# One order of three engines changed: a layer's value products ahead of the query projection, its block transposes behind the next maxima

## The chip, the cores and the metric

The kernel runs on one core of a Trainium2 chip. The metric is the device time of one execution in microseconds. A core has five engines that run their own instruction streams and meet through semaphores: TensorE (PE in the profile; PEld is its weight loads), VectorE (DVE), ScalarE (ACT), GpSimd (POOL) and SyncE (SP, which here issues the DMAs). TensorE writes only to PSUM, which has eight banks; ACT and DVE read results from there.

## The reference, cut to what matters

The output is x plus a dense low-rank attention of the normalised x plus a stack of six layers. The change lies in the layers alone, so only they are shown. T is 2048 tokens, a layer has 16 heads of 64, a local attention over windows of 32 tokens (each sees its own window and the one before), and a gated feed-forward part.

```
def attn_layer(x, Wqkv, qs, ksc, Wo):
    qkv = x @ Wqkv
    q, k, v = jnp.split(qkv, 3, -1)
    q = l2norm(q) * qs
    k = l2norm(k) * ksc
    q = q * cos * scale + rotate_half(q) * sin * scale
    k = k * cos * inv + rotate_half(k) * sin * inv
    out = local_attention(q, k, v)
    return out @ Wo
...
for i in range(DEPTH):
    x = attn_layer(shift_tokens(x), Wqkv[i], q_scale[i], k_scale[i], Wo[i]) + x
    x = ffn_layer(shift_tokens(x), ln_g[i], ln_b[i], W1[i], b1[i], W2[i], b2[i]) + x
```

## The kernel before

The first third of the time (part A of the kernel) is the dense attention. Part B, from about 770 us on, is the six layers. A layer is cut into 16 tiles of 128 tokens, 96 tiles in all, and the feed-forward part into chunks of four tiles. Each engine runs one hand-written loop over a turn number `u`; in every turn it does one step each for several tiles at different stages. On PE, turn `u` makes the scores of tile u-3, the q, k and v projections of tile u-1, the values' products (probabilities times v) and the output product of tile u-5, and the transposes of q and k ("turns", `L1342`) of tile u-2. Every engine works through its list strictly in the written order, so a wait of one step holds all steps written behind it.

The lines that matter, by engine:

- PE: scores `L1362` (mask `L1357` ahead of them), projections `L1316` to `L1318` (six matmuls each for q, k and v, `w_qkv` and `x_cut` in the name), values `L1378` (64 matmul records), output `L1390`, turns `L1342` (four transposes each: k_turn0, q_turn0, q_turn1, k_turn1, in that order), mean `L1399`, feed-forward products `L1316` with `xl_cut`, down product `L1429`.
- ACT: squares of q and of k `L754`, values_out `L796` (copies the values' bank to `o_T`), 16 exponentials `L805`, q_T `L776` and k_T `L785`/`L788`, v `L815`, gelu `L882`.
- DVE: maxima of the scores `L1069`, blocks `L1061` (a 32 by 32 transpose of the probabilities, `pc<-pr`), rotation of q or k: cosine `L1038`, sums of squares `L1020`, two sine halves `L1049`, `L1050`; residual `L1093`/`L1094`, sums of the probabilities `L1076`, deviation from the mean `L1101`, gate `L1147`.
- SP: eight DMAs `L471` carry the blocks to `xy`, from which the values' products read.

PSUM banks are given out by a table, and whoever takes a bank waits until its last user is read out:

```
BANKS = {"q": ((4, 5), (4, 5)), "k": ((2, 3), (2, 3)), "v": ((0, 1), (4, 5)),
         "q_turn0": ((4,), (4,)), "q_turn1": ((1,), (5,)), "k_turn0": ((6,), (6,)),
         "k_turn1": ((0,), (7,)), "values": ((6, 7), (6, 7)), "output": ((7,), (7,)),
         "score": ((0, 1), (0, 1)), "mean": ((7,), (7,)), "var": ((4,), (4,)),
         "up0": ((4, 5), (4, 5)), "up1": ((2, 3), (2, 3)), "up2": ((6, 7), (6, 7)),
```

Two of its consequences are used below. q_turn0 takes bank 4 right after q of the same turn, so it waits for `q_out`, the second sine half of q's rotation on DVE. And the values take banks 6 and 7, whose last user is up2 of the feed-forward part (read by the gate on DVE, `up_out2`), the mean (read by the deviation on DVE, `mean_out`), the down product or the output, in turns of four.

A chunk's steps fall into four kinds of turn, which repeat: a turn with the mean (A below), one with variance and down product (B), one without any (C), one with the three up products (D). The round read below is A from 1647.69 us, B from 1661.23, C from 1676.69 and D from 1690.19 to 1706.65, each from one start of the scores to the next.

Of the kernel before, what the change touches and what calls it, by code (L numbers as in the profile page):

```python
# [100 lines left out]
def tile(x):  # L101
    return x if 0 <= x < END else None


def chunk(x):
    c, r = divmod(x - 3, 4)
    return c if r == 0 and 0 <= c < CHUNKS else None


def dense_turn(x):  # L110
    g, r = divmod(x - 22, 8)
    return g if r == 0 and 0 <= g < NC else None


def late(x):
    c = chunk(x)
    return c if c is not None and c >= CHUNKS - NC else None
# [15 lines left out]
def bank_users():  # L133

    users, last = {}, {}

    def take(stage, unit):
        if unit is not None:
            of = BANKS[stage][unit % 2]
            users[stage, unit] = [last[b] for b in of if b in last]  # L140
            last.update({b: (stage, unit) for b in of})

    for u in range(FIRST, LAST):
        take("score", tile(u - 3))
        take("finish", late(u - 12))
        take("q", tile(u - 1))
        take("values", tile(u - 5))
        take("k", tile(u - 1))
        take("output", tile(u - 5))
        take("k_turn0", tile(u - 2))  # L150
        take("q_turn0", tile(u - 2))
        take("q_turn1", tile(u - 2))
        take("mean", chunk(u - 5))
        take("k_turn1", tile(u - 2))
        take("v", tile(u - 1))
        take("up0", chunk(u - 8))
        take("up2", chunk(u - 8))
        take("var", chunk(u - 6))
        take("down", chunk(u - 10))
        take("att", dense_turn(u))  # L160
        take("up1", chunk(u - 8))
    return users
# [583 lines left out]
def scalar_b(e, w, m, s):  # L746
    banks = Banks(m, s)

    def squares(u, i):
        if u is None:  # L750
            return
        w.wait_ge(s[f"proj{i}"], u + 1)
        w.wait_ge(s[f"ss{i}"], u)
        e.activation(m.nrms[i][:, :].rearrange("p (a b) -> p a b", a=2), banks.two("qk"[i], u),  # L754
                     ACT.Square).then_inc(s[f"sq{i}"], 1)

    def root_estimate(u):
        if u is None:
            return
        r = m.rs[u % 2]  # L760
        w.wait_ge(s["q_scaled"], u - 1)
        w.wait_ge(s["k_scaled"], u - 1)
        w.wait_ge(s["rB_arg"], u + 1)
        e.activation(r[1][:, :], r[0][:, :], ACT.Ln).then_inc(s["rB_ln"], 1)
        w.wait_ge(s["rB_ln"], u + 1)
        e.activation(r[2][:, :], r[1][:, :], ACT.Exp, scale=-0.5).then_inc(s["rB_exp"], 1)
        w.wait_ge(s["rB_exp"], u + 1)
        e.activation(r[1][:, :], r[2][:, :], ACT.Square).then_inc(s["rB_sq"], 1)

    def turned_q(u, hf):  # L770
        if u is None:
            return
        bank = banks.one(f"q_turn{hf}", u).rearrange("p (a b) -> p a b", b=P)
        w.wait_ge(s[f"turn0{hf}"], u + 1)
        w.wait_ge(s["score_mm"], u)
        e.activation(m.q_T[:, 4 * hf:4 * hf + 4, :], bank, ACT.Copy).then_inc(s[f"qT_out{hf}"], 1)  # L776
# [14 lines left out]
    def values_out(u):  # L791
        if u is None:
            return
        w.wait_ge(s["pv_mm"], u + 1)
        w.wait_ge(s["y_mm"], u)
        e.activation(m.o_T[:, :, :].rearrange("p (g j) i -> p g (j i)", g=2), banks.two("values", u), ACT.Copy).then_inc(s["oT_out"], 1)  # L796
# [96 lines left out]
    for u in range(FIRST, LAST):  # L893
        exponentials(tile(u - 4))
        squares(tile(u - 2), 1)
        turned_q(tile(u - 3), 0)
        turned_q(tile(u - 3), 1)
        turned_k(tile(u - 3), 0)
        turned_k(tile(u - 3), 1)
        keep_v(tile(u - 2))  # L900
        deviation_squares(chunk(u - 6))
        high_ln(chunk(u - 8))
        ln_root_estimate(chunk(u - 7))
        dense_output(dense_turn(u - 1))
        gelu_table(chunk(u - 9))
        gelu(chunk(u - 9), 0)
        high_x(tile(u))
        gelu(chunk(u - 9), 1)
        gelu(chunk(u - 9), 2)
        root_table(chunk(u - 9))  # L910
        scale_shift(chunk(u - 8))
        root_estimate(tile(u - 2))
        squares(tile(u - 1), 0)
        values_out(tile(u - 5))

# [92 lines left out]
def vector_b(e, w, m, s):  # L1010
# [19 lines left out]
    def rotate_cos(u, i):  # L1030
        if u is None:
            return
        n, raw = "qk"[i], banks.two("qk"[i], u).rearrange("p a (h d) -> p (a h) d", d=DH)
        w.wait_ge(s[f"sq{i}"], u + 1)
        w.wait_ge(s["rt"], u + 1)
        w.wait_ge(s[f"turn{i}0"], u - 1)
        w.wait_ge(s[f"turn{i}1"], u - 1)
        e.tensor_tensor(view(m.tcs[u % 2][i][:, :]), raw, wide(m.rt[u % 2][:, 2 * i, :], DH), ALU.mult).then_inc(s[f"rot{n}_c"], 1)  # L1038
# [17 lines left out]
    def blocks(u):  # L1056
        if u is None:
            return
        w.wait_ge(s["pnorm"], u + 1)
        w.wait_ge(s[f"moved{u % 2}"], 128 * (u // 2))  # L1060
        e.transpose(m.pc[u % 2][:, :, :, :].rearrange("p w h c -> p (w h) c"),  # L1061
                    m.pr[u % 2][:, :, :, :].rearrange("p w h c -> p (w h) c")).then_inc(s["pT"], 1)

    def maxima(u):
        if u is None:
            return
        w.wait_ge(s["score_mm"], u + 1)
        w.wait_ge(s["smexp"], u)
        e.tensor_reduce(m.mxB[:, 0, :], banks.two("score", u).rearrange("p a (b c) -> p (a b) c", c=2 * WIN), AX.X, ALU.max,  # L1069
                        negate=True).then_inc(s["sm_max"], 1)  # L1070
# [126 lines left out]
    for u in range(FIRST, LAST):  # L1197
        gated(chunk(u - 9), 2)
        final_sum(late(u - 11))
        ln_root_slope(chunk(u - 7))  # L1200
        maxima(tile(u - 3))
        rotate_cos(tile(u - 1), 0)
        square_sums(tile(u - 1), 0)
        rotate_sin(tile(u - 1), 0)
        ln_root_fix(chunk(u - 7))
        residual_1(tile(u - 5))
        prob_sums(tile(u - 3))
        low_ln(chunk(u - 8))
        rotate_cos(tile(u - 1), 1)
        prob_reciprocals(tile(u - 3))  # L1210
        rotate_sin(tile(u - 1), 1)
        if u == 6:
            sums_reciprocal()
        dense_norm(dense_turn(u))
        final_add(late(u - 11))
        square_sums(tile(u - 1), 1)
        root_argument(tile(u - 1))
        gated(chunk(u - 8), 0)
        gated(chunk(u - 8), 1)
        deviation(chunk(u - 5))  # L1220
        add_epsilon(chunk(u - 6))
        blocks(tile(u - 3))
        residual_2(chunk(u - 10))
        first_scale(chunk(u - 6))

# [86 lines left out]
def tensor_b(e, w, m, s):  # L1312
# [7 lines left out]
    def project(u, which):  # L1320
        if u is None:
            return
        bank, xc = banks.two("qkv"[which], u), m.x_cut[u % 2]
        w.wait_ge(s["x_hi"], u + 1)
        w.wait_ge(s["x_lo"], u + 1)
        w.wait_ge(s[f"ld_wqkv{which}"], 32 * (u // NT + 1))
        banks.wait_free(w, "qkv"[which], u)
        for hf in range(2):
            o = which * INNER + hf * CH
            mm = cut_product(bank[:, hf, :], [xc[:, k, :] for k in range(2)], [m.w_qkv[:, k, o:o + CH] for k in range(2)])  # L1330
        mm.then_inc(s[f"proj{which}"], 1)
# [107 lines left out]
    def finish(c):  # L1439
        if c is None:  # L1440
            return
        bank = banks.one("finish", c).rearrange("p (j f) -> p j f", f=P)
        w.wait_ge(s["fin_sum"], c % NC + 1)
        banks.wait_free(w, "finish", c)
        for j in range(CH // P):
            o = c % NC * CH + j * P
            t = e.transpose(bank[:, j, :], m.att[:, o:o + P], m.ident[:, :])
        t.then_inc(s["fin_T"], 1)

    for u in range(FIRST, LAST):  # L1450
        score(tile(u - 3))
        finish(late(u - 12))
        project(tile(u - 1), 0)
        values(tile(u - 5))
        project(tile(u - 1), 1)
        output(tile(u - 5))
        turn(tile(u - 2), 1, 0)
        turn(tile(u - 2), 0, 0)
        turn(tile(u - 2), 0, 1)
        mean(chunk(u - 5))  # L1460
        turn(tile(u - 2), 1, 1)
        project(tile(u - 1), 2)
        up_product(chunk(u - 8), 0)
        up_product(chunk(u - 8), 2)
        variance(chunk(u - 6))
        down_product(chunk(u - 10))
        dense_output(dense_turn(u))
        up_product(chunk(u - 8), 1)
# [62 lines left out]
```

## Time and profile before

| what | value |
|---|---|
| runs (three) | median 2306.8 us, 2303.33 to 2308.38 |
| profiled execution, its own time | 2294.56 us |
| its span, first to last instruction | 2292.8 us |
| granted TensorE clock, mean of the span | 0.971 of full speed |
| PE / DVE / ACT / POOL busy | 92% / 86% / 77% / 57% of the span |
| tiles, values' products, block transposes | 96 each |

The table is read so: the span is what the trace covers, the profiled execution lies 12 us below the median of the runs, and a busy share is a mean over both parts. A busy share of PE counts modelled ends of pipelined matmuls, so two neighbours overlap in the rows, and the start of the next one says more than the end of the last.

### The profile page before, as it was taken

The page shows a single profiled execution, that of the slowest core. Times are in us where ns is not written, and L with a number is a line of the kernel's source. Part 1 is how long each engine was busy: PE and PEld are TensorE (multiplying, and loading weights), DVE is VectorE, ACT ScalarE, POOL GpSimd, SP SyncE. Part 2 cuts the span into 40 slices and gives each one's busy share as a digit, 9 for nine tenths or more (in the row PEclk, how much of TensorE's full clock was granted, in tenths as well). Part 3 has the DMA queues.
Part 4 walks back from the last instruction along what each step waited for, and adds up shares of the span by engine and source line. Part 5 has one row for each costly group of instructions (what it writes and reads, how often), then busy time and mean ns, then how long its engine had stood idle before and what let it go on. Part 6 is the DMA issues. An engine that isn't in the chain of part 4 may idle for free. (4 is left out here: it accounts for less than half of the span.)

```text
span 2292.8 us, 69755 instructions
## 1 busy us (share of the span) xinstructions
PE 2105.6 (92%) x28217; PEld 1292.7 (56%) x28313; DVE 1981.1 (86%) x2378; ACT 1774.5 (77%) x4234; POOL 1316.2 (57%) x1088
## 2 busy tenths in 40 slices
PE   5999999999997689999999999999999999899985
PEld 2122222222222467777777777776777777777773
DVE  7999999999990789988998989888898989898973
ACT  3388888888887478878878878887887888788873
POOL 4211111111100888887877878788787888788860
PEclk8699999999999799999999999999999999999998
DMA  2322222222220233343425333433334433433331
GB/s 44 96 65 78 72 73 78 70 82 49 60 69 16 54 84 85 93 128 95 102 72 142 94 93 88 130 98 82 85 92 116 104 88 85 125 88 100 90 79 41
DMA packets 167654, 194.06 MB, mean 85 GB/s; under 512 B 87398, under 2 KB 107364, under 8 KB 167332
## 3 DMA queue, kind: packets, MB, share of 16 engines
q1 hardware_dynamic: 167076, 189.59, 31.5%
q8 instruction: 223, 3.65, 0.7%
q14 instruction: 99, 0.81, 0.1%
q10 hardware_dynamic: 256, 0.00, 0.0%
HBM read 56.91 MB, written 25.42 MB: 36 GB/s over the span
## 5 line engine op out<-in xcount | busy, mean ns | idle before, releaser
L988 DVE TENSOR_REDUCE mx<-S_ps 128x1 f32<-128x1024 f32 x512 | 601.6, 1219 | 24.8 <-PE S_ps L1270 19.1
L736 ACT ACTIVATE PT<-E_ps 128x512 f32<-128x512 f32 x1024 | 533.4, 602 | 101.4 <-PE E_ps L1279 98.9
L642 POOL TENSOR_TENSOR tc<-tc,ts 128x1024 f32<-128x1024 f32 x192 | 464.4, 2419 | 34.5 <-DVE ts L1050 34.0
L650 POOL TENSOR_TENSOR tc<-tc,rs 128x1024 f32<-128x1024 f32 x192 | 362.0, 1907 | 13.8
L1270 PE MATMUL S_ps<-KS,QS 48*128 48x512 bf16 x1024 | 320.5, 399 | 9.9 <-DVE mx L988 4.7
L805 ACT ACTIVATE pr<-B_ps,mxB 128x64 f32<-128x64 f32 x1536 | 325.0, 372 | 2.6 <-DVE mxB L1069 2.6
L1279 PE MATMUL E_ps<-QS,KS 64*128 64x512 bf16 x1024 | 316.8, 382 | 7.4 <-ACT PT L736 5.2
L584 POOL CAST w_cut_b<-w_raw_b 128x512 fp32r<-128x512 f32 (+1 forms) x48 | 27.6, 576 | 511.3 <-DMA w_raw_b<-in_Wqkv 379.1
L1316 PE MATMUL B_ps<-w_qkv,x_cut 128*128 128x512 f32 x576 | 260.9, 453 | 26.1 <-POOL x_cut L597 9.2
L1038 DVE TENSOR_TENSOR tc<-B_ps,rt 128x1024 f32<-128x1024 f32 x192 | 234.8, 1223 | 45.2 <-ACT nrm L754 31.9
L1287 PE MATMUL O_ps<-PT,va 128*32 128x512 f32 x2048 | 273.7, 606 | 0.0
L1279 PEld LDWEIGHTS E_ps<-QS,KS 64*128 64x128 bf16 x1024 | 79.3, 93 | 338.2 <-ACT PT L736 259.0
L604 POOL TENSOR_TENSOR pr<-pr,mxB 128x1024 f32<-128x1024 f32 x96 | 184.0, 1917 | 142.2 <-DVE mxB L1083 142.2
L754 ACT ACTIVATE nrm<-B_ps 128x1024 f32<-128x1024 f32 x192 | 208.6, 1086 | 54.0 <-PE B_ps L1318 52.0
L1318 PE MATMUL B_ps<-w_qkv,x_cut 128*128 128x512 f32 x576 | 231.7, 402 | 0.4 <-issue 0.4
L1317 PE MATMUL B_ps<-w_qkv,x_cut 128*128 128x512 f32 x576 | 232.1, 403 | 0.0
L1020 DVE TENSOR_REDUCE ss<-nrm 128x16 f32<-128x1024 f32 x192 | 232.0, 1208 | 0.0
L1342 PE MATMUL B_ps<-ident,tc 128*128 128x128 f32 x1536 | 202.2, 277 | 23.4 <-DVE ts L1050 9.3
L1378 PE MATMUL B_ps<-xy,vs 128*64 128x64 f32 x3072 | 195.0, 227 | 21.2 <-issue 11.1
L1342 PEld LDWEIGHTS B_ps<-ident,tc 128*128 128x128 f32 x1536 | 172.7, 142 | 51.1 <-issue 19.0
L1378 PEld LDWEIGHTS B_ps<-xy,vs 128*64 128x64 f32 x3072 | 166.6, 140 | 58.0 <-issue 57.9
L1390 PEld LDWEIGHTS B_ps<-o_T,w_o 128*128 128x128 f32 x1536 | 187.6, 193 | 14.1 <-ACT o_T L796 6.2
(179 smaller groups left out, 3982.0 us busy)
## 6 DMA issues: line engine op xcount, KB each, us to landing
xy<-pc SPq DMA_DIRECT2D x768, 64.0 KB, 2.0
vs<-v SPq DMA_DIRECT2D x96, 384.0 KB, 3.7
Wqkv_cut<-w_cut_b SPq DMA_DIRECT2D x72, 256.0 KB, 2.4
w_qkv<-Wqkv_cut SPq DMA_DIRECT2D x36, 512.0 KB, 7.2
rot<-in_rot SPq DMA_DIRECT2D x96, 128.0 KB, 2.6
vs<-v SPq DMA_DIRECT2D x96, 128.0 KB, 3.8
w_raw_b<-in_Wqkv SPq DMA_DIRECT2D x36, 256.0 KB, 2.9
W_cut<-w_cut_b SPq DMA_DIRECT2D x24, 170.5 KB, 2.5
```

Source lines behind the costliest of these rows:

```text
L642: e.tensor_tensor(tc[:, :], tc[:, :], m.ts[i][:, :], ALU.add).then_inc(s[f"rot{n}"], 1)
L650: e.tensor_tensor(tc, tc, m.rs[u % 2][2][:, i * H:(i + 1) * H].unsqueeze(2).to_broadcast([P, H, DH]), ALU.mult).then_inc(s[f"{n}_scaled"], 1)
L736: e.activation(m.PT[n % NPT][:, :], turns.bank("probs", n)[:, :], ACT.Exp).then_inc(turns.sem("probs", n), 1)
L805: a = e.activation(pb[:, :, h, :], sc[:, h, :, :], ACT.Exp, bias=m.mxB[:, 0, h:h + 1], scale=1.0)
L988: e.tensor_reduce(m.mx[h % 2][:, i, hf:hf + 1], m.S_ps[n % 2][:, :, :], AX.XY, ALU.max).then_inc(s["sc_max"], 1)
L1038: e.tensor_tensor(view(m.tcs[u % 2][i][:, :]), raw, wide(m.rt[u % 2][:, 2 * i, :], DH), ALU.mult).then_inc(s[f"rot{n}_c"], 1)
L1270: mm = e.matmul(m.S_ps[n % 2][:, c, :], m.QS[sl][rows, i * P:(i + 1) * P], m.KS[sl][rows, k:k + CH], start=True, stop=True)
L1279: e.matmul(turns.bank("probs", n)[:, :], m.KS[sl][rows, j * P:(j + 1) * P], m.QS[sl][rows, chunk_cols(c)], start=True, stop=True).then_inc ...
L1287: e.matmul(m.O_ps[VC * c:VC * (c + 1), :], m.va[:, j, h, :], m.PT[n % NPT][:, :], start=(j == 0), stop=(j == NT - 1)).then_inc(s["pv"], 1)
L1316: e.matmul(bank, left[0], right[0], start=True, stop=False)
L1342: t = e.transpose(bank[:, j, :], m.tcs[u % 2][i][:, b * P:(b + 1) * P], m.ident[:, :])
L1378: mm = e.matmul(bank[at, j, :, b, :], v[:, d:d + DH], m.xy[u % 2][:, b, :, par * NP + j, :], start=(b == 0 and j % (NP // 2) == 0), stop=T ...
```

## The change

Four lists are rewritten, with no instruction added or removed. PE makes the values' products right behind the scores, and q's and k's projections stand next to each other behind them; the table of bank users follows. ACT copies the values out before it squares q. DVE does the block transpose of a tile one place later, behind the maxima of the next tile.

```
 def bank_users():
...
         take("score", tile(u - 3))
         take("finish", late(u - 12))
+        take("values", tile(u - 5))
         take("q", tile(u - 1))
-        take("values", tile(u - 5))
         take("k", tile(u - 1))
...
 def scalar_b(e, w, m, s):
...
         root_estimate(tile(u - 2))
+        values_out(tile(u - 5))
         squares(tile(u - 1), 0)
-        values_out(tile(u - 5))
...
 def vector_b(e, w, m, s):
...
         maxima(tile(u - 3))
+        blocks(tile(u - 4))
         rotate_cos(tile(u - 1), 0)
...
         add_epsilon(chunk(u - 6))
-        blocks(tile(u - 3))
         residual_2(chunk(u - 10))
...
 def tensor_b(e, w, m, s):
...
         score(tile(u - 3))
         finish(late(u - 12))
+        values(tile(u - 5))
         project(tile(u - 1), 0)
-        values(tile(u - 5))
         project(tile(u - 1), 1)
```

On PE, this is the order in a turn of kind A before, from the scores to the second transposes of q; the brackets name the semaphores that a row waits for.

```order
L1362 MATMUL B_ps<-k_T,q_T 32x64 x64
L1316 MATMUL B_ps<-w_qkv,x_cut 128x512 [waits up_out0,x_lo,x_hi]
...
L1378 MATMUL B_ps<-xy,vs 64x2x32 [waits up_out2,shift1,moved1]
...
L1316 MATMUL B_ps<-w_qkv,x_cut 128x512 [waits up_out1]
...
L1390 MATMUL B_ps<-o_T,w_o 128x128 [waits oT_out]
...
L1342 MATMUL B_ps<-ident,tc 128x128 [waits k_scaled]
...
L1342 MATMUL B_ps<-ident,tc 128x128 [waits q_out,q_scaled]
...
L1342 MATMUL B_ps<-ident,tc 128x128 [waits smexp]
```

The two `L1316` rows are q's and k's projection. This is the same piece of the changed kernel.

```order
L1362 MATMUL B_ps<-k_T,q_T 32x64 x64
L1378 MATMUL B_ps<-xy,vs 64x2x32 [waits up_out2,shift1,moved1]
...
L1316 MATMUL B_ps<-w_qkv,x_cut 128x512 [waits up_out0,x_lo,x_hi]
...
L1316 MATMUL B_ps<-w_qkv,x_cut 128x512 [waits up_out1]
...
L1390 MATMUL B_ps<-o_T,w_o 128x128 [waits oT_out]
...
L1342 MATMUL B_ps<-ident,tc 128x128 [waits k_scaled]
...
L1342 MATMUL B_ps<-ident,tc 128x128 [waits q_out,q_scaled]
...
L1342 MATMUL B_ps<-ident,tc 128x128 [waits smexp]
```

The values moved up by one projection, with their wait for `up_out2`; between q's projection and the row that waits for `q_out` there now stand only k's projection, the output product and one set of transposes.

On DVE, these are the rows from the end of a turn of kind D into one of kind A before: gate, blocks, gate, maxima and the rotation of q.

```order
L1147 SCALAR_TENSOR_TENSOR hid<-B_ps,b,gel 128x512 [waits gelu1]
L1061 STREAM_TRANSPOSE pc<-pr 128x1024 [waits moved0,pnorm]
L1147 SCALAR_TENSOR_TENSOR hid<-B_ps,b,gel 85x512 [waits gelu2]
L1069 TENSOR_REDUCE mxB<-B_ps 128x16 [waits score_mm]
L1038 TENSOR_TENSOR tc<-B_ps,rt 128x1024 [waits turn00,turn01,rt,sq0]
```

And this is the same place in the changed kernel.

```order
L1147 SCALAR_TENSOR_TENSOR hid<-B_ps,b,gel 128x512 [waits gelu1]
L1147 SCALAR_TENSOR_TENSOR hid<-B_ps,b,gel 85x512 [waits gelu2]
L1069 TENSOR_REDUCE mxB<-B_ps 128x16 [waits score_mm]
L1061 STREAM_TRANSPOSE pc<-pr 128x1024 [waits moved0,pnorm]
L1038 TENSOR_TENSOR tc<-B_ps,rt 128x1024 [waits turn00,turn01,rt,sq0]
```

The block transpose moved behind the third gate and the maxima; the rotation of q still waits for its squares (`sq0`) from ACT.

## Rows read from the trace of the kernel before

**Rows 1.** Stretches A, B, D, sum: length, busy PE PEld DVE ACT POOL, clock, DMA.

```profile
1647.69:1661.23 13.54, 13.06 (x246) 10.50 (x246) 11.85 (x17) 12.23 (x32) 10.12 (x9) 1.00 0.36 90
1661.23:1676.69 15.46, 15.40 (x253) 11.71 (x253) 14.18 (x20) 11.36 (x32) 14.20 (x13) 1.00 0.32 80
...
1690.19:1706.65 16.46, 16.39 (x263) 13.22 (x263) 14.69 (x20) 14.57 (x37) 14.97 (x13) 1.00 0.30 75
sum 58.96, PE 57.31 PEld 45.58 DVE 54.07 ACT 50.23 POOL 50.10; mean PE 14.33 PEld 11.39 DVE 13.52 ACT 12.56 POOL 12.52
```

**Rows 2.** Timeline of PE in turn A: start, length, instruction, [idle before].

```profile
1649.11 0.50 PE L1316 MATMUL B_ps<-w_qkv,x_cut 128*128 128x512 f32 x1
...
1650.75 0.34 PE L1378 MATMUL B_ps<-xy,vs 128*64 128x64 f32 x4
...
1652.77 0.50 PE L1316 MATMUL B_ps<-w_qkv,x_cut 128*128 128x512 f32 x1
...
1654.27 1.95 PE L1390 MATMUL B_ps<-o_T,w_o 128*128 128x128 f32 x16
...
1660.93 0.38 PE L1357 MATMUL B_ps<-mask_bf,ident_bf 128*128 128x512 bf16 x1 [0.33 <-ACT k_T L788]
```

**Rows 3.** Timeline of PE in turns C and D.

```profile
1687.60 0.50 PE L1316 MATMUL B_ps<-w_qkv,x_cut 128*128 128x512 f32 x1 [0.31 <-ACT q_T L776]
...
1689.88 0.38 PE L1357 MATMUL B_ps<-mask_bf,ident_bf 128*128 128x512 bf16 x1 [0.62 <-ACT k_T L788]
...
1692.87 0.40 PE L1318 MATMUL B_ps<-w_qkv,x_cut 128*128 128x512 f32 x1
...
1695.21 0.50 PE L1316 MATMUL B_ps<-w_qkv,x_cut 128*128 128x512 f32 x1
...
1698.52 1.95 PE L1342 MATMUL B_ps<-ident,tc 128*128 128x128 f32 x16
```

**Rows 4.** Timeline of DVE, end of turn A's rotation and the same in D.

```profile
1654.73 0.68 DVE L1050 TENSOR_TENSOR ts<-B_ps,rt 128x512 f32<-128x512 f32 x1
1656.25 0.28 DVE L1093 TENSOR_TENSOR stream<-B_ps,stream 64x128 f32<-64x128 f32 x1 [0.84 <-PE B_ps L1390]
...
1657.22 1.22 DVE L1076 TENSOR_REDUCE mxB<-pr 128x16 f32<-128x1024 f32 x1 [0.37 <-ACT pr L805]
...
1662.76 0.69 DVE L1101 TENSOR_TENSOR xl<-stream,B_ps 128x512 f32<-128x512 f32 x1 [0.18 <-issue]
...
1697.23 0.68 DVE L1050 TENSOR_TENSOR ts<-B_ps,rt 128x512 f32<-128x512 f32 x1
```

**Rows 5.** Timeline of DVE around the block transpose between D and A.

```profile
1648.74 1.24 DVE L1061 STREAM_TRANSPOSE pc<-pr 128x1024 f32<-128x1024 f32 x1
1649.90 0.71 DVE L1147 SCALAR_TENSOR_TENSOR hid<-B_ps,b,gel 85x512 f32<-85x512 f32 x1
```

**Rows 6.** Timeline of ACT in turn A.

```profile
1647.35 1.49 ACT L882 ACTIVATE gel<-B_ps,b 128x512 f32<-128x512 f32 x2 [0.17 <-PE B_ps L1318]
```

**Rows 7.** Timeline of DVE, a late rotation of q in another turn.

```profile
1376.82 0.68 DVE L1050 TENSOR_TENSOR ts<-B_ps,rt 128x512 f32<-128x512 f32 x1
```

**Rows 8.** Timeline of PE, waits of two kinds elsewhere in part B.

```profile
1377.65 1.50 PE L1342 MATMUL B_ps<-ident,tc 128*128 128x128 f32 x12 [1.68 <-DVE ts L1050]
...
2033.60 0.34 PE L1378 MATMUL B_ps<-xy,vs 128*64 128x64 f32 x4 [1.34 <-DVE xl L1101]
```

**Rows 9.** Timeline of PE in the first turn of a layer.

```profile
1726.77 0.27 PE L1378 MATMUL B_ps<-xy,vs 128*64 128x64 f32 x1 [2.91 <-issue]
```

**Rows 10.** Busy time by stretch after two long stalls of PE (columns as in group 1).

```profile
1726.80:1730.70 3.90, 3.90 (x58) 3.49 (x59) 1.42 (x3) 1.37 (x4) 3.90 (x3) 0.61 0.80 194
1862.00:1867.00 5.00, 2.66 (x67) 2.28 (x66) 4.97 (x4) 1.16 (x2) 4.69 (x5) 1.00 0.58 110
```

**Rows 11.** Timeline of DVE near the end of part B.

```profile
2226.49 1.25 DVE L1061 STREAM_TRANSPOSE pc<-pr 128x1024 f32<-128x1024 f32 x1 [0.50 <-POOL pr L604]
...
2232.48 1.23 DVE L1069 TENSOR_REDUCE mxB<-B_ps 128x16 f32<-128x1024 f32 x1
```

More of the change, by code:

```diff
@@ L145, in bank_users @@
         take("finish", late(u - 12))
+        take("values", tile(u - 5))
         take("q", tile(u - 1))
-        take("values", tile(u - 5))
         take("k", tile(u - 1))
@@ L912, in scalar_b @@
         root_estimate(tile(u - 2))
+        values_out(tile(u - 5))
         squares(tile(u - 1), 0)
-        values_out(tile(u - 5))
 def vector_a(e, w, m, s):
@@ L1201, in vector_b @@
         maxima(tile(u - 3))
+        blocks(tile(u - 4))
         rotate_cos(tile(u - 1), 0)
@@ L1221, in vector_b @@
         add_epsilon(chunk(u - 6))
-        blocks(tile(u - 3))
         residual_2(chunk(u - 10))
@@ L1452, in tensor_b @@
         finish(late(u - 12))
+        values(tile(u - 5))
         project(tile(u - 1), 0)
-        values(tile(u - 5))
         project(tile(u - 1), 1)
```

## The prediction

> **What bounds the kernel now.** I read first the busy times of four neighbouring turns, because the six layers are one round of four turns said again and again. A turn runs from one start of the scores to the next; A, B, C and D are named in the text ahead. TensorE is busy for 57.31 of the round's 58.96 us, VectorE for 54.07, so PE is the nearest to a bound, and DVE has 4.89 us to spare [rows 1]. Second, I read PE's timeline for what it stands at. In B and D it hardly stands at all (15.40 of 15.46 and 16.39 of 16.46 [rows 1]), so there whatever holds PE is paid in full. In A and C it waits shortly before the next scores for ACT's copies of k (0.33 in A, 0.62 in C), and in C for the copies of q too (0.31) [rows 2, 3]: there a stall of PE can in part be taken out of these waits. Third, I read DVE's and ACT's timelines in the same turns for what PE's banks are waiting for, and last two places of part B where such a wait already happens.
>
> **The change part by part.** No instruction is added. The price, if any, is in waits.
>
> *The query's bank.* q_turn0 takes bank 4 from q of the same turn, and waits until DVE has done the second sine half of q's rotation. In turn D, q's last matmul ends at 1692.87 + 0.40 = 1693.27 [rows 3] and that sine half at 1697.23 + 0.68 = 1697.91 [rows 4]. So the chain squares on ACT, cosine, sums, two sine halves on DVE takes 4.64 us. How soon PE goes on after it is seen where PE did wait for it: the sine half ends at 1376.82 + 0.68 = 1377.50 [rows 7], the transposes start at 1377.65 [rows 8], 0.15 later. On PE, from the start of k's projection (1695.21) to q_turn0 pass 3.76 us: k_turn0 starts at 1698.52, and its four of 16 transposes in 1.95 us take 0.45 [rows 3]. Before the change, the values' products stood between q's end and k's start, 2.02 us (1650.75 to 1652.77 [rows 2]), and the chain was just covered. After it, k starts right behind q. A product of six matmuls takes 1.50 (1652.77 to 1654.27 [rows 2]), 0.25 each, and the last one is 0.40 long [rows 3], so q ends 0.15 after k's start. q_turn0 then starts 0.15 + 4.64 + 0.15 = 4.94 after k's start instead of 3.76: **1.18 us later in each turn**. From this goes the seam between q and values: q's product lasts 1.64 to the start of the values (1649.11 to 1650.75), k's 1.50 [rows 2], so 0.14 may be saved where values no longer follow a projection; it may also come back behind the scores, where no row shows such a seam. I take it as saved, 1.04 net; the bounds are 1.04 and 1.18.
>
> *What is left of it.* In D all of it, 1.04. In C, PE's waits of 0.31 and 0.62 hide most, and 0.2 is left (bounds 0 and 1.18).
>
> *Values ahead of q in A.* The values take banks 6 and 7 from up2, and wait for the third gate on DVE. The block transpose no longer stands ahead of that gate (1648.74 [rows 5]); its gelu ends at 1647.35 + 1.49 = 1648.84 [rows 6], the gate takes 0.71 [rows 5], and with the 0.15 the values can start at 1649.70. The scores leave PE at 1649.11, where q started [rows 2]. So PE stands 0.59 where q's projection used to cover the wait. k then starts at 1649.70 + 2.02 + 1.50 = 1653.22 instead of 1652.77, 0.45 later, and q_turn0 0.45 + 1.18 = 1.63 later. PE's 0.33 ahead of the next scores hides a part, which leaves between 0.45 and 1.30. I take the middle, 0.9.
>
> *Values ahead of q in B.* Here they take bank 7 from the mean, so they wait for the deviation on DVE, a wait that another turn of B shows already, 1.34 us long [rows 8]. With k at 1653.22 in A, q's end is 1653.37 and q's rotation ends at 1658.01, where it ended at 1654.73 + 0.68 = 1655.41 [rows 4]. Behind it come the two residual adds (0.28 and about as much) and the sums of the probabilities, now at 1658.6 instead of 1657.22, 1.4 later. From there to the deviation DVE has no gap but 0.18 [rows 4], so the deviation ends at 1662.76 + 0.69 + 1.4 = 1664.85, and the values can start at 1665.0. The scores of B leave PE 13.54 [rows 1] after those of A, at 1662.65, and 0.9 later now, at 1663.55. PE stands 1.45. Together with the 1.04 of the query's bank, B is longer by 2.5 (bounds 1.04 and 3). ACT's copy of the values has a whole projection more time, so the output product loses nothing.
>
> *Maxima ahead of blocks.* The maxima start up to 1.24 sooner, the transpose's length [rows 5], and gain nothing: ACT's exponentials stand behind the squares of q, which now come last (before: behind values_out, in the same place). The blocks come later by the maxima and by what stands between, up to two ops of the feed-forward part. They feed the values two turns on, through eight DMAs; the moves and the first use lie more than a turn apart, so I cost it at nothing, and at up to 2 us in each of B's turns if that cover is gone. SP's loads of rotation tables and of a new layer's weights stand behind these moves and come about 2 us later, but so does the projection that needs them.
>
> *Ends.* In the first turn of a layer PE stands 2.91 us anyway between q and k (it stands at nothing that the profile shows, while weights load) [rows 9]. This covers B's 2.5 in five turns: -12.5. Near the end the blocks of the last tile but one move from 2226.49 behind the maxima at 2232.48 [rows 11], 6 us; the tail's values feel some of it: between 0 and 6, I take 3.
>
> *Sum.* A round: 0.9 + 2.5 + 0.2 + 1.04 = 4.64. Values and q share a turn in 92 turns (96 tiles; the first four turns have no values, the last four no q), 23 rounds: 106.7. Less 12.5, plus 3: 97. Against the profiled execution's own 2294.6 that is 2391.6. The runs shown have their median 12.2 above that execution, so I put the 97 on the median: 2306.8 + 97 = **2404 us**, 4.2% slower.
>
> A rule to weigh against this: PE is busy for 57.31 us of the round, its weight loads for 45.58 and DVE for 54.07 [rows 1]. The Trainium skill, Perfetto Trace Analysis, section Identifying the Most-Contended Engine, says that the busy share of matmuls is a poor measure, that weight loads should be taken instead, and that the engine with the highest occupancy is the one that counts. By that rule DVE is the bound here, and a change that adds no work to it costs only what its 4.89 us of idle time can't take up; the sum would then be near 0. The rows of B and D, in which PE never stands, speak against reading it so.
>
> **The rivals.**
>
> *Only the bank, no waits of the values.* If DVE and ACT run ahead again by the next turn, the values find their banks free: A 0.45, B 1.04, C 0.2, D 1.04, 2.7 a round, 62 in 23 rounds, less 5 in the first turns of layers, plus 3: 60, 2367. For it: in D nothing waits for such a bank. Against it: DVE's sums start 1.4 later by its own order.
>
> *No change.* DVE takes up what is lost: the two long holds of A and B, 0.59 + 1.45 of PE and the 2 x 1.18 behind, come to 4.4, which fits into DVE's 4.89 [rows 1]. This needs PE to be ahead of DVE on the average, so that a hold moves idle time and adds none: 2307. Against it: PE stands nowhere in B and D.
>
> *Faster.* The seam of 0.14 is saved in 92 turns, 13 us, and the query's rotation is through in time: 2294. That needs the chain of 4.64 to shrink below 3.46 (3.76 less 0.15 and 0.15). DVE's part can start sooner, since the blocks wait no longer ahead of it, but in turn D it starts right behind the squares, so nothing of the kind is free. The price decides from 1.2 us on.
>
> *Clock.* After a stall of 2.91 us [rows 9] the granted clock of the next 3.9 us is 0.61, so it fell to its lower level, 1.2 GHz, for most of it; a stretch with 2.34 us of standing, 2.66 busy of 5.00, kept 1.00, 2.4 GHz [rows 10]. If the new stalls of B bring the clock down in each round, the stretch of 3.9 us loses 0.39 of itself, 1.5 us: 23 x 1.5 = 35 more, 2440. The Trainium skill, TensorE: Matmul & The Clock Gate, section Why this matters for your kernels, warns of idle gaps between bursts of matmuls in this way. [...]
>
> **How the numbers follow.** Chances: the forecast (2380 to 2425) 0.55; only the bank (2345 to 2380) 0.2; clock, or more waits (above 2425) 0.12; slightly slower (2312 to 2345) 0.03; no change 0.05; faster 0.05. The range 2350 to 2435 takes in the forecast, most of the bank's case and the nearer part of the clock's, 0.8 in all. A measurement of this kernel can tell about 0.2% from no change, 4.6 us. So slower 0.9, same 0.05, faster 0.05. The cases of slower hold most of the chance, and the range is theirs.
>
> **What the profile would show.** Right: PE's transposes wait in nearly every turn for DVE's second sine half, 1.0 to 1.2 us; the values in A wait for a gate and in B for the deviation; turns B and D grow by about 2.5 and 1.0, C hardly; ACT waits for q's projection where it waited for the values. Wrong: if B and D keep 15.5 and 16.5, the chain behind q is shorter than I read it, or covered; if the values wait for the moved blocks instead, the transpose's new place is the cost; if the granted clock falls below 0.95, the clock is.

## The result, and the profile after

The changed kernel takes 2449.0 us (median of four runs, 2446.1 to 2453.7), the kernel before 2305.1 on the same chip: 1.0631 times as long, 95% interval 1.0612 to 1.0651. The forecast had the direction and 97 of the 144 us; the time lies 14 us above its range. The profiled execution takes 2453.7 us against 2294.6 before, 159 more, and the numbers from traces below are of that pair, or of the profiled execution of the run named.

The page of the changed kernel, its span, its busy times and the row of the queue that brings PE's instructions:

```profile
span 2451.9 us, 69851 instructions
...
PE 2124.0 (87%) x28313; PEld 1316.6 (54%) x28313; DVE 1991.2 (81%) x2378; ACT 1787.8 (73%) x4234; POOL 1312.5 (54%) x1088
...
q8 instruction: 223, 3.65, 0.6%
```

The busy time did not grow by what the span grew; every engine's share fell. So the time went into waiting. The same round as in [rows 1], A, B, C, D, each from scores to scores:

```profile
1745.18:1759.74 14.56, 12.93 (x248) 10.56 (x247) 11.45 (x15) 12.14 (x32) 9.90 (x9) 1.00 0.33 83
1759.74:1777.60 17.86, 15.54 (x253) 11.88 (x252) 14.65 (x21) 12.17 (x33) 14.78 (x13) 1.00 0.27 69
1777.60:1791.40 13.80, 12.22 (x246) 10.24 (x245) 12.38 (x17) 11.84 (x33) 9.13 (x9) 1.00 0.34 86
1791.40:1810.43 19.03, 16.68 (x264) 13.47 (x263) 15.91 (x21) 14.79 (x37) 15.79 (x13) 1.00 0.26 65
sum 65.25, PE 57.38 PEld 46.16 DVE 54.39 ACT 50.94 POOL 49.61; mean PE 14.34 PEld 11.54 DVE 13.60 ACT 12.73 POOL 12.40
```

PE's work is the same to 0.1 us (57.31 before, 57.38 now) and the clock column stays at 1.00; the round is longer by 6.3. What PE stands at, in this round:

```profile
1747.12 0.34 PE L1378 MATMUL B_ps<-xy,vs 128*64 128x64 f32 x4 [0.46 <-DVE hid L1147]
...
1755.60 1.06 PE L1342 MATMUL B_ps<-ident,tc 128*128 128x128 f32 x8 [1.18 <-DVE ts L1050]
...
1762.36 0.34 PE L1378 MATMUL B_ps<-xy,vs 128*64 128x64 f32 x4 [1.14 <-DVE xl L1101]
...
1787.49 1.50 PE L1342 MATMUL B_ps<-ident,tc 128*128 128x128 f32 x12 [1.17 <-DVE ts L1050]
...
1790.87 0.59 PE L1357 MATMUL B_ps<-mask_bf,ident_bf 128*128 128x512 bf16 x2 [0.40 <-ACT k_T L788]
...
1794.60 0.27 PE L1378 MATMUL B_ps<-xy,vs 128*64 128x64 f32 x2 [1.05 <-issue]
...
1802.60 1.50 PE L1342 MATMUL B_ps<-ident,tc 128*128 128x128 f32 x12 [1.18 <-DVE ts L1050]
```

Five of the seven rows are waits that were forecast: the values in A for the third gate, the query's transposes in A, C and D for the second sine half, the values in B for the deviation. The wait for the copies of k, ahead of the next scores in C, stood there before. The row that is put down to issue was not forecast. In D the values have begun, and stop in their middle for 1.05 us at nothing that the profile shows. Selected rows of PE's waits over all of part B, first before the change, then after (columns: who waited for whom, us in total, times, longest):

```profile
PE B_ps L1357 <- ACT k_T L788: 19.4, 42, 0.6
PE B_ps L1378 <- issue: 14.4, 11, 3.1
...
PE B_ps L1342 <- DVE ts L1050: 9.3, 5, 2.6
PE B_ps L1362 <- issue: 8.7, 7, 1.8
```

```profile
PE B_ps L1342 <- DVE ts L1050: 110.6, 91, 2.6
PE B_ps L1378 <- issue: 40.1, 34, 3.8
PE B_ps L1378 <- DVE xl L1101: 23.0, 22, 3.2
PE B_ps L1362 <- issue: 16.8, 8, 3.2
PE B_ps L1378 <- DVE hid L1147: 16.0, 23, 2.5
...
PE B_ps L1357 <- ACT k_T L788: 7.6, 19, 0.4
```

The two rows for the copies of k can't be compared as they stand. Two matmuls with the mask stand ahead of each scores; the trace of the kernel before has a record of only one of them (95 records of `L1357` in part B, where the changed kernel's has 190), so each of its rows counts some 0.22 us of a matmul without a record as idle. The 0.62 of C in [rows 3] and the 0.40 above are the same wait.

The waits inside scores and values put down to "issue" come in 42 pieces instead of 18. The table gives only the part in which PE is idle. Measured as excess of the scores over their undisturbed 1.27 us from first to last start, and of the values over 1.86, between the first and the last scores, these pauses are 31.5 us before and 78.8 after: 47.3 more.

**What the pauses are.** The trace has 57159 instructions of PE's program (28313 matmuls, as many weight loads, 531 semaphore waits and two others). Counted out along it, every one of the 36 pauses over 0.25 us inside the values and the 8 over 0.35 inside the scores begins at place 193 or 194 of a stretch of 256, and so do the 12 and 7 before the change; not one begins elsewhere. 57159 is 223.3 times 256, and queue q8 moved 223 pieces, 3.65 MB, 16 KB each. One of them, the only transfer of any queue in the 1.2 us from 2050.0 (that stretch's DMA view), and the pause behind it in PE's timeline of a turn C:

```profile
DMA packets 1, 0.02 MB, mean 14 GB/s; under 512 B 0, under 2 KB 0, under 8 KB 0
...
q8 instruction: 1, 0.02, 5.2%
```

```profile
2051.27 0.29 PE L1378 MATMUL B_ps<-xy,v 128*64 128x64 f32 x4
2052.59 0.28 PE L1378 MATMUL B_ps<-xy,vs 128*64 128x64 f32 x3 [1.03 <-issue]
```

The piece moves from 2050.09 to 2051.09, and PE goes on at 2052.59. All of these pauses end 1.2 to 1.6 us after the end of such a piece. So the theory is that PE runs out of instructions: it uses up 256 faster than the next 256 come. The scores with their masks are 260 instructions in 1.4 us, the values 128 in 2.0; before the change q's projection, 12 instructions in 1.64 us, stood between these two dense runs.

The rival is that the change only moved the border of the 256 into worse places. The counts speak against it: before the change 55 borders fall inside the values, and PE pauses for over 0.25 us at 12 of them; after it 49 fall there, and it pauses at 36. Each scores has one border in either kernel, with 7 and 8 pauses.

That instructions are 64 bytes long, as 16384 / 256 is here, is what the Trainium skill says in Trainium Architecture — The Big Picture, section The software stack; it has the streams brought to the engine when a program is loaded. The rows differ: 223 pieces come while the kernel runs.

### The profile page after: what moved, and what is told of

Same layout as the page of the kernel before. It is cut to its first block and busy times, and to the rows that moved or that the text cites. A ratio compares the mean times of both kernels' runs of the same rounds, so it can differ in the third digit from the quotient of the medians.

```text
span 2451.9 us, 69851 instructions
## 1 busy us (share of the span) xinstructions
PE 2124.0 (87%) x28313; PEld 1316.6 (54%) x28313; DVE 1991.2 (81%) x2378; ACT 1787.8 (73%) x4234; POOL 1312.5 (54%) x1088
## 3 DMA queue, kind: packets, MB, share of 16 engines
q8 instruction: 223, 3.65, 0.6%
## 5 line engine op out<-in xcount | busy, mean ns | idle before, releaser
L650 POOL TENSOR_TENSOR tc<-tc,rs 128x1024 f32<-128x1024 f32 x192 | 361.7, 1905 | 13.8
L1342 PE MATMUL B_ps<-ident,tc 128*128 128x128 f32 x1536 | 207.6, 277 | 115.9 <-DVE ts L1050 110.6
L1316 PE MATMUL B_ps<-w_qkv,x_cut 128*128 128x512 f32 x576 | 252.9, 439 | 18.9 <-POOL x_cut L597 9.5
L1378 PE MATMUL B_ps<-xy,vs 128*64 128x64 f32 x3072 | 206.7, 232 | 71.5 <-issue 26.9
L754 ACT ACTIVATE nrm<-B_ps 128x1024 f32<-128x1024 f32 x192 | 209.3, 1090 | 70.7 <-PE B_ps L1318 70.6
L1378 PEld LDWEIGHTS B_ps<-xy,vs 128*64 128x64 f32 x3072 | 178.4, 144 | 85.3 <-issue 76.2
L796 ACT ACTIVATE o_T<-B_ps 128x1024 f32<-128x1024 f32 x96 | 98.6, 1027 | 170.5 <-PE B_ps L1378 170.5
```

The source lines that it names most:

```text
L650: e.tensor_tensor(tc, tc, m.rs[u % 2][2][:, i * H:(i + 1) * H].unsqueeze(2).to_broadcast([P, H, DH]), ALU.mult).then_inc(s[f"{n}_scaled"], 1)
L1316: e.matmul(bank, left[0], right[0], start=True, stop=False)
L1342: t = e.transpose(bank[:, j, :], m.tcs[u % 2][i][:, b * P:(b + 1) * P], m.ident[:, :])
L1378: mm = e.matmul(bank[at, j, :, b, :], v[:, d:d + DH], m.xy[u % 2][:, b, :, par * NP + j, :], start=(b == 0 and j % (NP // 2) == 0), stop=T ...
```

## The experiments

**Moving PE's stream against the 256.** Idle waits on a semaphore that is long raised are put into PE's list, two to an instruction, so that the border of the 256 falls at the same place of every round. In the changed kernel good is 131 to 157 instructions behind the start of the values, that is behind their end; bad is 49 to 75, in their middle. The two differ only in the first number, 120 or 202.

```
+PAD_FIRST, PADS = 120, {9: 8, 10: 8, ... 96: 3}
...
     for u in range(FIRST, LAST):
+        for _ in range(2 * (PAD_FIRST if u == FIRST else PADS.get(u, 0))):
+            e.wait_ge(s["mask"], 1)
         score(tile(u - 3))
```

Good, expected: 

> The changed kernel with idle waits put into PE's list (120 ahead of part B, 4 to 6 per turn, all on a semaphore that is long raised), so that every 256th instruction of PE's stream falls behind the values' products in all turns. Theory fetch (the stalls of 0.3 to 4 us inside scores and values are PE waiting for the next 16 KB of its instructions): nearly all of the 80 us of such stalls go, 2370 to 2395 us, and the rows of the values have no idle time put down to issue but in a few turns. Rival (the stalls come from late data, from weight loads or the clock): the position of the stream does not matter, 2449 give or take 10, the same as the run with the other position.

Bad, expected: 

> The same kernel with the same number of idle waits per turn and 202 instead of 120 ahead of part B, so that every 256th instruction of PE's stream falls into the values' products in all turns. Theory fetch: every round pays about 0.5 in A and B, 1.6 in C and 1.3 in D, and 3 to 4 in the first turn of a layer, 100 to 110 us in all instead of 80: 2460 to 2490, and 80 to 110 above the run with the good position. Rival: no difference between the two, 2449 give or take 10.

The kernel before in the good position, expected: 

> The kernel before with the same idle waits as the good position. Theory fetch: it loses the 33 us of such stalls that it has itself, 2270 to 2285. Rival: 2307 give or take 5.

Measured, against 2301.9 us of the kernel before: good 2405.6 (ratio 1.0439, 1.0408 to 1.0469), bad 2512.8 (1.0926, 1.0907 to 1.0945), before in the good position 2296.4 (0.9983, 0.9967 to 0.9999). Good and bad lie 107 us apart; they have the same steps, data and waits in the same order, and differ in 82 idle instructions ahead of part B. The pauses inside the values in PE's waits, good and then bad (the added line moves line numbers by one):

```profile
PE B_ps L1343 <- DVE ts L1051: 108.8, 88, 2.7
...
PE B_ps L1379 <- issue: 2.7, 3, 1.2
```

```profile
PE B_ps L1343 <- DVE ts L1051: 111.6, 94, 2.6
PE B_ps L1379 <- issue: 88.5, 75, 4.2
```

The wait for the sine is the same in both. All three took longer than expected, by 11, 23 and 11 us: the idle waits ahead of part B put off the first scores, 120 instructions from 769.3 to 779.1 us, 202 to 788.7, some 80 to 95 ns for each instruction with its two waits. From the first to the last scores, free of that:

| kernel | us, first to last scores | excess inside scores and values |
|---|---|---|
| before | 1458.9 | 31.5 |
| after | 1612.5 | 78.8 |
| before, good | 1451.4 | 6.8 |
| after, good | 1558.1 | 8.1 |
| after, bad | 1650.9 | 121.0 |

After less before is 153.6. In the good position it is 106.7. The difference, 46.9, is what the excess says: 78.8 - 31.5 = 47.3, less 8.1 - 6.8 = 1.3, makes 46.0. So at this position the cost of the change falls into two parts that can be read apart, and the further runs are all in a good position. Not every pause that goes is gained: before loses 24.7 us of them and becomes 7.5 shorter, since PE then waits for a new layer's weights (12.3 us instead of 3.2) and for POOL ahead of the transposes (13.4 instead of 2.9); after loses 70.7 and becomes 54.4 shorter. That 46.9 and 46.0 agree rests on these two losses, 17.2 and 16.3, being alike. The changed kernel was not run in the position of the last experiment below, which is better for the kernel before.

**The deviation earlier on DVE.**

```
         rotate_sin(tile(u - 1), 1)
+        deviation(chunk(u - 5))
...
-        deviation(chunk(u - 5))
         add_epsilon(chunk(u - 6))
```

Expected: 

> The changed kernel in the good position (2406 us) with the deviation from the mean ahead of the sums of k's squares on DVE, 1.5 us sooner. Theory values' wait in B: the 24 us in which the values wait for the deviation go, 2380 to 2390. Rival (the wait moves to the next bank or to the query's sine): 2400 or more.

2399.0 us, 6.6 less than the good position and much less than the theory. The runs can't tell it from nothing: against the kernel before on the same chip the ratios are 1.0428 (1.0408 to 1.0447) and 1.0439 (1.0408 to 1.0469). The trace shows the step itself: the values' wait for the deviation is gone from PE's waits, and B's median fell from 17.51 to 17.06, but the wait for q's sine stays (111.9 us, 108.8 in the good position), and PE waits 12.9 instead of 8.6 for a new layer's weights.

**The block transposes back.**

```
-        blocks(tile(u - 4))
...
         add_epsilon(chunk(u - 6))
+        blocks(tile(u - 3))
```

Expected: 

> The changed kernel in the good position (2406 us) with the block transposes back at their old place on DVE. Theory third gate: the transpose stands ahead of the third gate again, 1.24 us, and the values of A wait for that gate 1.2 longer: 23 times 0.9 to 1.2, 2425 to 2435. Rival (the place of the transposes costs and gives nothing): 2400 to 2411.

2429.6 us, 24 more, as expected. The values' rows in PE's waits:

```profile
PE B_ps L1378 <- DVE hid L1147: 40.3, 23, 3.3
PE B_ps L1378 <- DVE xl L1101: 23.9, 23, 3.2
PE B_ps L1378 <- DVE stream L1161: 17.3, 21, 0.9
```

The gate is waited for 40.3 us instead of 16.0. In C a wait of 17.3 for the feed-forward residual comes in as well, which stands behind the transposes too; by the median A is 1.12 us longer and C 0.91. So this part of the change is a gain within it.

**ACT in the old order.**

```
-        values_out(tile(u - 5))
         squares(tile(u - 1), 0)
+        values_out(tile(u - 5))
```

Expected: 

> The changed kernel in the good position (2406 us) with ACT's two steps in the old order, squares of q ahead of the copy of the values. The output product then waits for that copy, some 0.7 us a turn, which the wait for the sine behind it (1.17) takes up: 2400 to 2415. If the order on ACT carries the change: 2450 or more.

2419.1 us, 13 more. The output product waits 58.8 us for the copy of the values, and the wait for the sine, which ends at the same time as ever, shrinks to 30.2 from 108.8. One wait swallowed the other, as expected; the 13 stand 4 us outside the expectation. The traces show them behind the transposes: in C v's projection starts 0.61 us later, and the waits for the copies of q (6.2 us in 20 turns) are there again, which the good position doesn't have; those for the copies of k are 19.2 instead of 11.1. By the median C is 0.62 longer, A 0.38, and B 0.26 shorter (the two profiled executions are only 5.7 apart). So the new order on ACT is a gain within the change too.

**The sine halves first.**

```
         rotate_cos(tile(u - 1), 0)
+        rotate_sin(tile(u - 1), 0)
         square_sums(tile(u - 1), 0)
-        rotate_sin(tile(u - 1), 0)
```

Expected: 

> The changed kernel with its instruction stream in the good position (2406 us), and DVE's two sine halves of q ahead of the sums of q's squares, so that q's bank comes free 1.2 us sooner. Theory bank: the 109 us in which the transposes of q wait for the sine go nearly all; B and D gain 1.2 a round each, A about 0.85, C 0.3 (the rest comes back as waits for ACT's copies): 3.2 to 3.5 a round, 75 to 85 in all, 2320 to 2340. Rival (DVE sets the pace, its shifted work makes PE wait elsewhere): at most 20 gained, 2385 or more.

With the deviation earlier too, expected: 

> Both of the two edits above. If the two terms add: 2297 to 2320, about what the kernel before takes with its stream in the good position (2296). If one wait hides behind the other: 2320 to 2340, no better than the sine alone.

Both missed: 2435.2 and 2434.1 us, 28 to 30 slower than the good position. DVE and POOL in a turn C of the first of them, and the same DVE step in the good position:

```profile
1773.59 2.36 POOL L642 TENSOR_TENSOR tc<-tc,ts 128x1024 f32<-128x1024 f32 x1 [1.44 <-DVE ts L1050]
...
1774.47 2.04 DVE L1130 SCALAR_TENSOR_TENSOR xl<-lnv,xl 128x512 f32<-128x512 f32 x1
```

```profile
1759.82 0.68 DVE L1131 SCALAR_TENSOR_TENSOR xl<-lnv,xl 128x512 f32<-128x512 f32 x1
```

POOL's addition of q's two parts starts as soon as the sines are done, and the DVE step that now falls beside it takes 2.04 instead of 0.68 us (median of the 24 chunks, 22 of them over 2). It seems to do its work only when POOL is through: POOL ends at 1775.95, and the step at 1776.51, 0.56 later. In the following turn D the transposes of k wait for POOL. The next two runs put that step (`ln_root_fix`) ahead of the cosine, where DVE waits for ACT.

```
+        ln_root_fix(chunk(u - 7))
         rotate_cos(tile(u - 1), 0)
```

Without and with the earlier deviation, expected: 

> As the run with the sine halves first (2435 us), and the op that took 2.06 instead of 0.68 us there beside POOL's addition (ln_root_fix on DVE) ahead of the cosine, where DVE waits for ACT anyway. Theory bank plus clash: both waits go, 2320 to 2345 us. Rival (the chain of POOL and DVE behind the rotation needs the time wherever the op stands): 2400 to 2435.

> The same with the deviation from the mean ahead of the sums of k's squares too. If the terms of the query's bank and of the values' wait in B are what the change cost beside the instruction fetch and the wait in A: 2300 to 2330, within 1 to 2 percent of the kernel before. Rival: 2395 or more.

The kernel before with the three edits on DVE, expected: 

> The kernel before in the good position (2296 us) with the three edits on DVE (sine halves first, ln_root_fix ahead of the cosine, deviation earlier). PE waits only 12 us for the sine there and nowhere for these ops else: 2280 to 2300.

2391.8 and 2383.2 us, 14 and 22 less than the good position, and for the kernel before 2331.1, 35 more than in its good position (its transposes wait 40.0 us for POOL instead of 13.4). All three miss their expectations. Moving the step gave back the loss of the run ahead (43 us between the two), but did not end the collision: at its new place it meets another operation of POOL (`L650`), and takes 1.07 us by the median in the first of these runs and 1.84 in the kernel before, again ending some 0.55 us after POOL. PE's waits without the deviation:

```profile
PE B_ps L1378 <- DVE xl L1101: 32.5, 23, 3.5
PE B_ps L1342 <- DVE ts L1050: 32.4, 70, 2.5
PE B_ps L1342 <- POOL tc L650: 23.4, 23, 4.4
...
PE B_ps L1342 <- DVE stream L1094: 10.9, 24, 0.5
```

Of the 108.8 us for the sine 76 are gone, but the transposes now wait for POOL (7.2 in the good position) and for the residual add, which on DVE still stands behind the sums, and B's values wait longer. The query's bank could not be set free by this reordering without holding up what is next, so its price is read from the turns (below), and not shown by taking it away.

**A version that beats both.** The position is free to choose for the kernel before too. The idle waits go to the start of the kernel, where PE waits 14.6 us for its first data, and the border of the 256 lies ten instructions later.

```
 def tensor_a(e, w, m, s):
+    for _ in range(2 * PAD_FIRST):
+        e.wait_ge(s["ld_id"], 16)
```

Expected: 

> The kernel before with its stream in the good position, ten instructions further along in each turn, and the idle waits that set the position (110) at the very start of the kernel, where PE waits 14.6 us for its first data, not ahead of part B, where 120 of them moved the first scores by 9 us. Theory fetch: 7 us between the first and the last scores as in the first such run, some 3 more for the waits that were left in A and C there, and no delay of the first scores: 2285 to 2295, 0.3 to 0.7 percent below the kernel before. Rival (the position gives the kernel before nothing): 2297 to 2305.

2281.8 us against 2296.3, 0.9937 (0.9919 to 0.9955): faster than both kernels, with nothing but idle instructions added, and below the expectation. The profiled execution is the fastest of its runs, 2271.2 us. In it the excess inside scores and values is 0.4 us, and from the first to the last scores it takes 1432.4 us instead of 1458.9. Not all of the 26.5 need be pauses: in that stretch TensorE is granted 1.2 GHz for 3.4 us instead of 34.1, which at half speed is worth up to 15 us. How the gain is shared was not separated. One of its six runs took 4163.7 us and is not in the ratio; why was not found.

## Why the prediction was right in part, and where it failed

- **The query's bank: right.** The query's transposes were forecast to start 4.94 us behind k's projection and 1.04 later in the turn. In the good position, by the median of D, it is 4.96 and 1.12 (9.89 us behind the start of the scores instead of 8.77); of the seam of 0.14 some 0.10 is saved. PE stands 1.17 or 1.18 there, and the wait grew from 9.3 to 110.6 us, in 91 pieces.
- **The values in A and B: right, B a little too large.** Forecast 0.59 and 1.45, measured 0.46 and 1.14 in the round shown, on the gate and the deviation that were named.
- **The sum of a round: right, free of the fetch.** Between the two kernels in the good position, by medians of 16 to 21 turns of a kind outside the layers' first turns: A 1.01, B 2.09, C 0.29, D 1.31, sum 4.70. Forecast 0.9, 2.5, 0.2, 1.04, sum 4.64. The sum fits better than its parts: B's 0.41 too much makes up for the others. C comes out near the forecast, but not by the waits that were named. The wait for the copies of k, the larger of the two, gives nothing back: its row is 0.62 in C in both kernels in the good position, and 0.22 of it is the mask's matmul without a record, in [rows 2, 3] too. What is given back are two waits of the kernel before: that of the transposes for the exponentials (0.27, not named) and that of v's projection for the copies of q (0.49 from start to start, 0.31 in the row). So the 0.2 of C is in part luck. D is too small by 0.27: its transposes are 0.08 later than forecast, and the up products start almost 0.2 later again.
- **Ends, the five first turns of layers: the first step that failed.** They were to cover B's 2.5 each, -12.5. They grew by 4.35, 2.02, 1.08, 3.19 and 2.79, 13.4 in all. The pause of 2.91 in [rows 9], which was put down to the loading of weights, begins at place 193 of the 256, where the others begin too: it is the fetch. A wait whose cause was not known was taken as room for another one. In the good position these turns differ by 0.9 in all instead of five times 2.09, and PE waits for the layer's weights in them: without the fetch most of the cover is there.
- **The cost that was left out: the instruction fetch, 47 us.** This is the step that decided. The part on the values ahead of q priced their waits and their banks; that two runs of small matmuls now follow each other, and what holds an "issue" row, was not asked, although before's own 18 such pauses stood in the trace. It comes out mostly in C and D (1.09 and 2.24 by the mean, not 0.2 and 1.04) and in the five first turns of layers (13.4 instead of 0.9). That is where the pauses grew: PE's idle time put down to issue went from 8.3 to 20.2 us in C, from 1.9 to 18.0 in D, from 11.4 to 15.6 in B and from 2.7 to 5.6 in A.
- **The tail: right in size.** Forecast 3, the middle of a range of 0 to 6, and the last values come 3.5 us later behind the last scores.
- **Sum.** Free of the fetch the change costs 106.7 between the scores and 3.5 behind them, 110.2, where 97 was forecast; the larger part of the difference is in turns that are longer than the median of their kind. With 46.9 for the fetch, the first turns of layers included, this makes 157.1, where the profiled pair shows 159.1; the clock's share (below) is somewhere inside these terms.
- **The rivals.** The clock was not what the forecast feared, since the round runs at 1.00 through B's stalls. It did fall 16 times between the first and the last scores instead of 9, 71.7 us at 1.2 GHz instead of 34.1, each time in or behind a pause of 2.3 to 3.8 us (in the good position it is 44.4 and 30.7 us); at most half of the 37.6 is lost by that, a part of it stands in the excess already, and how the rest is shared between clock and waits stays open. That DVE takes the loss up, as the rule of the Trainium skill in the prediction (Perfetto Trace Analysis, section Identifying the Most-Contended Engine) would have it, is excluded by 153.6 us more between the first and the last scores with unchanged work.

## What to carry to other kernels

Long runs of very small matmuls can be bounded by how fast instructions come. Here two such runs side by side starved PE at 36 of 49 borders in the second one, and with a projection between them at 12 of 55; keep something slow between them, or count the program out in 256s and see where the borders fall. A row that waits for "issue" is a question and no slack: look whether such rows recur at one place of the instruction count before another cost is hidden in them. And a wait taken off one bank by a new order pays only as far as the next user in line, so list that one before pricing the gain.

## What was not expected of the hardware

- PE's instructions come during the run in 16 KB pieces, 256 each, and where PE pauses at a border, it does so until 1.2 to 1.6 us after the end of a piece. Where that border falls was worth 107 us of 2500 in one kernel.
- An idle instruction with two satisfied waits took 106 ns in PE's list by the median, where 120 stood in a row (738.8 to 751.7 us in the good position), and put off the first scores by some 82.
- A DVE step of 0.68 us on two SBUF operands took 2.04 beside POOL's addition. The Trainium skill, SBUF — State Buffer, section SBUF: two separate sides, says that DVE with two SBUF inputs and GpSimd hold one port pair in turn, each for a whole instruction; the trace agrees (started 0.88 us into POOL's 2.36, the step ends 0.56 us after POOL).
